# Conditional output tiles taken two at a time in an adaptive feed-forward layer, and the up weights split one sequence earlier

## What is computed

```
xc    = x[b] @ W_cond[ids[b]].T
gate  = top-2 of softmax(xc @ W_router.T), renormalised
lora  = ((xc @ A.T) * gate) @ B.T * 2.0
out   = x + xc @ W_base.T + bias + lora
```

## Time and profile before

| | us |
|---|---|
| median of 3 runs | 397.62 (397.47 to 397.65) |
| the profiled execution | 397.48 |
| its span in the trace | 395.7 |
| TensorE busy | 390.4 (99%) |
| VectorE busy | 301.7 (76%) |
| ScalarE busy | 184.0 (46%) |
| GpSimd busy | 39.9 (10%) |

### The profile page before, as it was taken

One profiled execution on the slowest core, in us unless ns is written; L12 is line 12 of the kernel. 1 busy time (PEld: TensorE's weight loads), 2 busy tenths in 40 slices (PEclk: granted clock), 3 DMA queues, 4 the chain that ended last, 5 costly groups with the idle time before them and its releaser, 6 DMA issues.

```text
span 395.7 us, 5686 instructions
## 1 busy us (share of the span) xinstructions
PE 390.4 (99%) x2186; PEld 332.5 (84%) x2186; DVE 301.7 (76%) x429; ACT 184.0 (46%) x281; POOL 39.9 (10%) x67
## 2 busy tenths in 40 slices
PE   7999999999999999999999999999999999999996
PEld 7888888888888888888888888888888888888885
DVE  4897966779699999974457786768868999998311
ACT  5877734748632444222146676256746224441000
POOL 0101100110000040021172000000000002201110
PEclk9999999999999999999999999999999999999999
DMA  7998872768430056485669877356083102642222
GB/s 260 397 352 287 309 279 84 262 214 297 157 106 0 28 181 181 169 282 197 217 215 368 339 244 241 108 174 234 17 274 113 40 0 83 189 156 81 80 80 80
DMA packets 21083, 72.96 MB, mean 184 GB/s; under 512 B 2816, under 2 KB 2832, under 8 KB 21056
## 3 DMA queue, kind: packets, MB, share of 16 engines
q1 hardware_dynamic: 15840, 55.58, 40.4%
q0 software_dynamic: 4928, 15.97, 11.4%
q10 hardware_dynamic: 288, 1.05, 0.7%
HBM read 64.20 MB, written 8.39 MB: 183 GB/s over the span
## 4 chain that ended last, share of the span: by engine, by line
PE 97%; DMA 1%; ACT 0%; DVE 0%; ACTq 0%; issue 0%
PE bank_x L783 30%; PE bank_x L787 15%; PE bank_y L768 9%; PE bank_y L770 9%; PE bank_y L769 9%; PE bank_x L770 8%; PE bank_x L769 8%; PE bank_x L768 8%; PE bank_y L827 2%; DMA raw<-x 1%; PE bank_y L847 0%; ACT x_hl L483 0%; DVE out_sb L577 0%; ACTq L340 0%; ACT wc_hl L483 0%
## 5 line engine op out<-in xcount | busy, mean ns | idle before, releaser
L783 PE MATMUL bank_x<-x_hl,wc_hl 128*128 128x512 f32 x512 | 128.9, 393 | 0.8 <-ACT wc_hl L483 0.8
L526 DVE TENSOR_TENSOR wc_hl<-raw,wc_hl 128x1024 fp32r<-128x1024 f32 x90 | 108.4, 1220 | 19.4 <-ACT wc_hl L465 19.4
L465 ACT CAST wc_hl<-raw 128x1024 fp32r<-128x1024 f32 x90 | 93.6, 1051 | 59.8 <-DVE raw L530 23.6
L783 PEld LDWEIGHTS bank_x<-x_hl,wc_hl 128*128 128x128 f32 x512 | 92.1, 189 | 18.0 <-ACT wc_hl L483 1.5
L787 PEld LDWEIGHTS bank_x<-x_hl,wc_hl 128*128 128x128 f32 x512 | 70.0, 190 | 5.1
L787 PE MATMUL bank_x<-x_hl,wc_hl 128*128 128x256 f32 x512 | 71.5, 282 | 0.0
L417 POOL DMA_DIRECT2D out<-out_sb x28 | 15.3, 545 | 250.5 <-DVE out_sb L577 229.2
L494 ACT COPY xc_low<-bank_x 128x256 f32<-128x256 f32 x64 | 23.6, 369 | 32.7 <-PE bank_x L787 32.7
L669 DVE TENSOR_TENSOR xp<-bank_x,xc_low 128x256 f32<-128x256 f32 x64 | 26.9, 420 | 15.5 <-ACT xc_low L494 14.7
L569 DVE SCALAR_TENSOR_TENSOR out_sb<-bank_x,bias_sb,out_sb 128x512 f32<-128x512 f32 x32 | 23.5, 746 | 18.1 <-PE bank_x L770 15.1
L770 PE MATMUL bank_x<-x_hl,wc_hl 128*128 128x512 f32 x96 | 37.4, 389 | 0.0
(11 more groups left out here) (86 smaller groups left out, 478.5 us busy)
## 6 DMA issues: line engine op xcount, KB each, us to landing
raw<-w_cond SPq DMA_DIRECT2D x62, 512.0 KB, 4.8
raw<-w_base SPq DMA_DIRECT2D x24, 512.0 KB, 5.7
out_sb<-x POOLq DMA_DIRECT2D x32, 256.0 KB, 5.5
raw<-x SPq DMA_DIRECT2D x14, 512.0 KB, 5.1
out<-out_sb POOLq DMA_DIRECT2D x28, 256.0 KB, 2.3
raw<-x ACTq DMA_DIRECT2D x2, 512.0 KB, 3.7
raw<-w_cond SPq DMA_DIRECT2D x4, 256.0 KB, 3.8
out<-out_sb SPq DMA_DIRECT2D x4, 256.0 KB, 2.0
```

Source lines behind the costliest of these rows:

```text
L465: nc.scalar.copy(split_dst(key, HI), split_src(key)).then_inc(hi_done, 1)
L526: nc.vector.tensor_tensor(split_dst(key, LO), split_src(key), split_dst(key, HI).bitcast(F32), ALU.subtract).then_inc(lo_done, 1)
L783: nc.tensor.matmul(ps[:], wc_hl[:, slot_of(s, t), HI, k], x_hl[:, s % 2, k].rearrange("p h n -> p (h n)"), start=(k == 0), stop=False)
```

## The change

PE, ACT and DVE take the conditional tiles by a new table: pairs of two, and in odd sequences the last two tiles singly. For a pair, PE issues the 8 wide matmuls of both tiles and then the 8 narrow ones of both. ACT does L of the first tile, the first tile's splits, L of the second, then C of both, then the second tile's splits; DVE does S, the first tile's splits, S, then X of both, then the second tile's splits. The last two tiles of a sequence keep their splits at the end. `b` is split at (1, 5) and `bd` at (1, 7); `gate_h` and `h_high` stand behind tile 3 and `h_low` behind tile 5. `gate_to_rows` stays behind tile 1. Sequence 0's first two tiles keep their own code on PE (`first_cond`).

```diff
+COND_TILES = [[(0, 1), (2, 3), (4, 5), (6, 7)], [(0, 1), (2, 3), (4, 5), (6,), (7,)]]
-RESIDENT = {(0, 5): [("a", 0, 0)], (2, 5): [("b", 0, 0)]}
+RESIDENT = {(0, 5): [("a", 0, 0)], (1, 5): [("b", 0, 0)]}
...
-    if (s, t) == (2, 6):
+    if (s, t) == (1, 7):
         items = items + [("bd", 0, 0)]
...
+def early_splits(s, tiles):
+    return step_splits(s, tiles[0]) if tiles[0] < KT - 2 else []
+def late_splits(s, tiles):
+    if tiles[0] < KT - 2:
+        return step_splits(s, tiles[1])
+    return step_splits(s, KT - 2) + step_splits(s, KT - 1) if tiles[-1] == KT - 1 else []
...
+                    for tiles in COND_TILES[s % 2]:
+                        for t in tiles:
+                            act.wait_ge(cond_done, s * KT + t + 1)
+                            nc.scalar.copy(xc_low[:, t % 2], bank_x[t % HT][:, TOK:]).then_inc(low_copied, 1)
+                            if t == tiles[0]:
+                                for key in early_splits(s, tiles):
+                                    hi(key)
+                        for t in tiles:
+                            act.wait_ge(xc_summed, s * KT + t + 1)
+                            nc.scalar.copy(xc_hl[:, t, HI, s % 2 * TOK:(s % 2 + 1) * TOK],
+                                           xp[:, s // 2 % 2, t, s % 2 * TOK:(s % 2 + 1) * TOK]).then_inc(xc_hi, 1)
+                        for key in late_splits(s, tiles):
                             hi(key)
-                        if s % GSEQS == 2 and t == 2:
+                        if s % GSEQS == 2 and tiles[0] == 2:
                             h_high(2 * g)
...
+                    for tiles in COND_TILES[s % 2]:
+                        for t in tiles:
+                            dve.wait_ge(low_copied, s * KT + t + 1)
...
+                            if t == tiles[0]:
+                                split(early_splits(s, tiles))
+                        for t in tiles:
+                            dve.wait_ge(xc_hi, s * KT + t + 1)
...
+                        split(late_splits(s, tiles))
-                        if s % GSEQS == 2 and t == 2:
+                        if s % GSEQS == 2 and tiles[0] == 2:
                             gate_h(2 * g)
-                        if s % GSEQS == 2 and t == 3:
+                        if s % GSEQS == 2 and tiles[0] == 4:
                             h_low(2 * g)
...
+            def cond(s, tiles):
+                for t in tiles:
+                    pe.wait_ge(hi_done, SPLIT["w", s, t])
...
+                    ps = cond_bank(s, t)
+                    for k in range(KT):
+                        wide(ps, s, t, k)
+                for t in tiles:
+                    pe.wait_ge(lo_done, SPLIT["w", s, t])
+                    for k in range(KT):
+                        mm = narrow(bank_x[t % HT], s, t, k)
+                    mm.then_inc(cond_done, 1)
```

More of the change, by code:

```diff
@@ L664, in _ @@
                 for s in range(GSEQS * g, GSEQS * (g + 1)):
[L665 to L677, removed]
-                        if s % GSEQS == 2 and t == 2:
+                    for tiles in COND_TILES[s % 2]:
+                        for t in tiles:
+                            dve.wait_ge(low_copied, s * KT + t + 1)
+                            nc.vector.tensor_tensor(xp[:, s // 2 % 2, t, s % 2 * TOK:(s % 2 + 1) * TOK],
+                                                    bank_x[t % HT][:, 0:TOK], xc_low[:, t % 2], ALU.add) \
+                                .then_inc(xc_summed, 1)
+                            if t == tiles[0]:
+                                split(early_splits(s, tiles))
+                        for t in tiles:
+                            dve.wait_ge(xc_hi, s * KT + t + 1)
+                            xc_of = xc_hl[:, t, :, s % 2 * TOK:(s % 2 + 1) * TOK]
+                            nc.vector.tensor_tensor(xc_of[:, LO], xp[:, s // 2 % 2, t, s % 2 * TOK:(s % 2 + 1) * TOK],
+                                                    xc_of[:, HI].bitcast(F32), ALU.subtract).then_inc(xc_lo, 1)
+                        split(late_splits(s, tiles))
+                        if s % GSEQS == 2 and tiles[0] == 2:
                             gate_h(2 * g)
-                        if s % GSEQS == 2 and t == 3:
+                        if s % GSEQS == 2 and tiles[0] == 4:
                             h_low(2 * g)
@@ L802, in first_cond @@
                         mm.then_inc(cond_done, 1)
[L804 to L815, removed]
+            def cond(s, tiles):
+                for t in tiles:
+                    pe.wait_ge(hi_done, SPLIT["w", s, t])
+                    if t == 0:
+                        pe.wait_ge(lo_done, SPLIT["x", s, 0])
+                        pe.wait_ge(lo_done, SPLIT["x", s, 1])
+                    ps = cond_bank(s, t)
[6 more added lines that the diff above has]
+                    mm.then_inc(cond_done, 1)
             def router(p):
@@ L900, in _ @@
                 for s in range(GSEQS * g, GSEQS * (g + 1)):
[L901 to L907, removed]
+                    for tiles in COND_TILES[s % 2]:
+                        if s == 0 and tiles[0] == 0:
+                            first_cond()
+                        else:
+                            cond(s, tiles)
+                        if s % GSEQS == 2 and tiles[0] == 0:
                             gate_to_rows(2 * g)
```

## The result

| | before | changed |
|---|---|---|
| median, 6 runs each on one chip | 397.55 us | 399.09 us (398.9 to 399.32) |
| ratio | | 1.0039, 95% interval 1.0028 to 1.0049 |
| profiled execution | 397.48 | 399.32 |
| its span | 395.7 | 397.5 |

The forecast was 398.6, slower, with the range 397.0 to 399.8.

A forecast was written before the change was run, and what follows sets the result against it. PE was taken to bound the kernel, busy 390.4 of 395.7 us, with DVE in reserve. PE's saving of 0.5 against waits of 1.3, 0.15 and 0.1 gave +1.05, so 398.6 us, range 397.0 to 399.8.

The forecast's parts named there:

- The saving on PE: On PE, 27 changes from narrow to wide matmuls go, at 0.02 us a pair: 0.5 us less, at most 0.8.
- The router's wait in sequence 1: PE's router in sequence 1 waits for the sum of tile 7, mainly at slice 7: 1.3 us (1.0 to 1.6).
- The last sum: DVE's S of tile 7 in sequence 1 ends at 54.76, seen by PE at 54.80; the router wants it at 53.51.
- the chain: ACT and DVE hand-overs in series in sequence 1, from tile 2's copy at 39.87 to tile 7's sum at 54.76.
- Sequence 5: Router of sequence 5, same hand-overs without `b`: sum seen at 53.67, a wait of 0.15 us (nothing to 0.5).
- The gate: Gate ready at 65.6, PE's transposes in sequence 2 want it at 66.2: hidden with 0.6 us to spare.
- Sequences 2 and 6: High split of the next sequence's weight tile 2 ends at 22.1 us, wanted at 22.2; charged 0.1 us in all.
- a weight tile comes late: First weight tile of sequences 2 and 6 comes late, lengthening the router's wait: 399.6 to 400.3 us; chance 0.13.
- The sum: All terms together: -0.5 + 1.3 + 0.15 + 0.1 = +1.05 us on 397.48, giving 398.5, as median 398.6.

The follow-up runs named there:

- half tiles: Kernel before, with PE taking each conditional tile in two halves (4 wide, 4 narrow, 4 wide, 4 narrow): 398.25 us, ratio 1.0015.
- b_only: Kernel before, with only `b` and `bd` moved to sequence 1: 397.85 us, ratio 1.0008 to before.
- pe_pairs: Changed kernel's PE pairs and place of `b`, but ACT and DVE tile by tile as in the kernel before: 397.90 us, ratio 0.9998.
- splits_first: Changed kernel, with both tiles' splits of a pair ahead of the two casts and low parts: 397.84 us, ratio 1.0006 to before.
- b_late: Changed kernel, with `b` split behind the last sum of sequence 1, between weight tiles 2 and 3 of sequence 2: 398.33 us, ratio 1.0015.
- b_back: Changed kernel, all pairs kept, with `b` and `bd` split in sequence 2 again: 400.80 us, ratio 1.0083 to before.
- odd01_pair: Changed kernel, with only tiles 0 and 1 of odd sequences taken as a pair: 397.36 us, ratio 0.9987 to before.
- even_again: Second run of pairs in even sequences only, odd ones tile by tile, `b` and `bd` in sequence 1: 397.58 us, ratio 0.9998 to before.
- odd45_single: Changed kernel, with tiles 4 and 5 of odd sequences taken singly by all three engines: 397.87 us, ratio 1.0004 to before.

## Why the prediction was right, point by point

- **The saving on PE**, 27 changes at 0.02, was 0.12 up to the first router and 0.14 in each two sequences after it: 0.54, as worked out (0.5). The reason given, one fixed price for every change, holds only for runs of 8 and 16; half tiles cost less per change. The Trainium skill (TensorE: Matmul & The Clock Gate, section Back-to-back issue gap) gives the gap of an isolated matmul by its columns alone, with no term for the matmul ahead. By that rule two tiles and a pair take the same; the measured 5.588 and 5.567 differ.
- **The router's wait in sequence 1** was forecast at 1.3 (1.0 to 1.6) and measured 1.46 to 1.5. The last sum was to end at 54.76; it ended at 55.49 on a clock that started 0.60 later, 54.89, and every earlier step of the chain came within 0.08 of the forecast. Two terms were short. The chain left out X of tile 6, behind which the last S stands (54.73 to 55.07), and its steps were short by hundredths: 0.13 together, of which PE's own 0.05 (router at 52.51 - 0.60 = 51.91, forecast 51.86) takes off a part. And PE's restart was left out: after its wait the last slice needed 0.36 (55.54 to 55.90) and not 0.24. That `b` alone makes no wait, and the PE order with `b` only a third of it, was shown (`b_only`, `pe_pairs`), and the series was undone directly (`splits_first`).
- **Sequence 5** was forecast at 0.15 and took 0.33: slice 7, due at 247.82, started at 248.07, 0.25 late, and the restart took the rest. Same mechanism, term too small by half.
- **The gate** was to be ready at 65.6 and hidden; it was, at 65.8 by the same clock, and not waited for. That it is next in line was shown (`b_late`: PE would have come 1.1 us earlier than in the changed kernel, counted from tile 2, and was 0.5 late).
- **Sequences 2 and 6** were charged 0.1 for a margin of 0.1 us. They cost nothing (-0.14 for sequences 2 and 3, all that PE saves). The changed kernel's margin at the pair (2, 3) of sequence 3 was small, but 0.25 and not 0.1: the first of ACT's two casts ends 1.05 behind 88.42, and PE wants it at 89.72.

```profile
88.42 2.00 ACT L473 CAST wc_hl<-raw 128x1024 fp32r<-128x1024 f32 x2
```
```profile
89.72 3.82 PE L793 MATMUL bank_x<-x_hl,wc_hl 128*128 128x512 f32 x16
```

In front of the same pair, `b_back` put one more split of 1.13, and the pair was 0.93 late.

- **The rival "a weight tile comes late"** did not happen: the 1.71 of the earlier trace rows has no counterpart, and the 0.9 us that ACT's L473 still waits for a weight DMA lie at the start (before the casts at 12.09 and 13.38; L465 waited as long there before). Why the 1.71 went was not tested; the pairs want tiles later too.
- **The sum** was +1.05 and from tile 2 on it was +1.20 and +1.28. Both waits were larger than forecast and the charge for sequences 2 and 6 was not needed, so errors of 0.3 and 0.1 partly cancelled. The measured medians differ by 1.54 (by 1.45 when run again). The profiles leave 0.2 to 0.3 of that to the stretch ahead of tile 2, which scatters by more; that this is chance was not shown.

## What to carry to other kernels

Where PE never waits, a change of its order can give it only what its own order costs, here 0.02 us per pair; check first how late the other engines' longest series of hand-overs then ends, from a common anchor, at the place where PE next wants all of it. If tiles are batched, batch the work that depends on nothing (here the splits) ahead of the casts that wait for the other engine, and let the last tiles in front of a consumer go singly. And when a wait is taken away, say which one stands behind it: here moving `b` back cost 2.7 us in sequence 3, and moving it behind the last sum gave back half a microsecond and put the next wait at the gate.

## What the runs showed of the hardware that was not expected

**The start scatters by 1.6 us.** Tile 2 of sequence 0 started between 12.62 and 14.25 in fourteen profiled executions with the same start code. The chain of the second execution of the changed kernel shows what made the latest one late (start us, us, what): before SP can issue the first weight tile, it loads a sequence's id from memory (L364), in two steps.

```profile
0.73 1.93 SPq L364
2.69 1.55 SPq L364
...
5.33 3.46 DMA raw<-w_cond
8.80 0.63 ACT wc_hl L491
```

In the first execution of the changed kernel the two steps took 0.85 and 1.41 us, and the load landed 0.8 us sooner. This execution is the exception: in the others whose chain holds these steps the first took 0.84 to 1.02 and the second 1.35 to 1.64, and in two of them (`odd01_pair`, `even_again`) PE also waited 0.2 and 0.4 for ACT's third weight tile. In before's profile this path was not even in the chain, which began with x's load. A comparison of a few tenths needs the stretch behind this start, or many runs.

**Wide matmuls take longer behind narrow ones.** Eight wide matmuls behind narrow ones take 1.84 us, behind wide ones 1.81. Two changes behind four narrow ones cost only 0.01 more than one behind eight (2.80 a tile against 2.79), and a run of 16 narrow ones takes 1.91 where two of 8 take 1.90. The cause was not tested.

**PE needs longer for the first matmuls after a wait.** Eight router matmuls take 0.24 us in the stream (1.88 / 8) and took 0.35 to 0.36 from their restart to the next instruction in the changed kernel, `b_back`, `b_late`, `pe_pairs`, `odd45_single` and `splits_first`. A forecast of a wait has to add these 0.12; the 24 matmuls of `lora_down` behind it gave back 0.04 to 0.05 (the router alone was 1.51 and 0.37 longer, the router with `lora_down` 1.46 and 0.33).
